# Two waits of a fused attention and feed-forward kernel made finer: the value product by channel block, the bias by head group

## The reference

```python
x = x + tanh(g_xattn) * attention(layernorm(x), ctx)     # 16 heads of 32 channels, ALiBi bias, exp / (1 + sum)
# feed-forward of the RWKV kind, on h = layernorm(x)
xr = mu_r * h + (1 - mu_r) * h_prev ; xk = mu_k * h + (1 - mu_k) * h_prev
r = sigmoid(xr @ W_r.T) ; k_act = square(relu(xk @ W_k.T))
x = x + tanh(g_ffn) * r * (k_act @ W_v.T)
```

## Time and profile before

| | us |
|---|---|
| median of 3 runs | 1499.18 |
| lowest and highest | 1497.6, 1499.49 |
| the profiled execution | 1499.1 |
| its span, first to last instruction | 1497.3 |
| outside the span | 1.8 |

### The profile page before, as it was taken

One profiled execution on the slowest core, in us unless ns is written; L12 is line 12 of the kernel. 1 busy time (PEld: TensorE's weight loads), 2 busy tenths in 40 slices (PEclk: granted clock), 3 DMA queues, 4 the chain that ended last, 5 costly groups with the idle time before them and its releaser, 6 DMA issues.

```text
span 1497.3 us, 32734 instructions
## 1 busy us (share of the span) xinstructions
PE 1358.7 (91%) x10864; PEld 1122.8 (75%) x10864; DVE 1161.3 (78%) x2889; ACT 878.0 (59%) x2928; POOL 722.2 (48%) x766
## 2 busy tenths in 40 slices
PE   7988899899989999999998989998898999889898
PEld 6877778677777877778786777777686777768677
DVE  4447868787887878798786879878687987868785
ACT  5247474655747475574747566473756657375662
POOL 0003465545545554545555465555556454555542
PEclk9999999999999999999999999999999999999999
DMA  8721001020101102010010202011020101011000
GB/s 271 213 75 46 12 29 51 0 77 0 57 21 28 49 0 77 0 57 21 28 49 9 68 0 57 21 37 40 14 63 0 57 21 57 21 28 50 1 30 28
DMA packets 53009, 65.95 MB, mean 44 GB/s; under 512 B 23024, under 2 KB 29168, under 8 KB 52976
## 3 DMA queue, kind: packets, MB, share of 16 engines
q1 hardware_dynamic: 52976, 65.52, 14.9%
HBM read 40.87 MB, written 24.64 MB: 44 GB/s over the span
## 4 chain that ended last, share of the span: by engine, by line
DVE 37%; PE 22%; issue 21%; POOL 9%; ACT 6%; DMA 4%; DVEq 1%; SPq 1%; POOLq 0%; ACTq 0%
PE rotating L402 16%; DVE probs L1043 7%; DVE diff L1105 4%; POOL square L1362 4%; DVE mix_k L1100 4%; PE score_bank L402 3%; DMA xs<-in_x_dram 3%; DVE square L1100 2%; DVE relu L1105 2%; DVE xs L1069 2%; DVE mask_in L1142 2%; DVE stats L1013 2%; POOL probs L1325 2%; ACT probs L778 2%; DVE norm L1022 2%
## 5 line engine op out<-in xcount | busy, mean ns | idle before, releaser
L778 ACT ACTIVATE probs<-probs,neg_max 128x120 f32<-128x120 f32 x1024 | 391.7, 387 | 32.9 <-DVE neg_max L1047 32.9
L1325 POOL TENSOR_TENSOR probs<-probs,recip 128x960 f32<-128x960 f32 x128 | 229.8, 1795 | 216.2 <-DVE recip L1058 216.2
L402 PE MATMUL rotating<-mixed_key,w_key 128*128 128x512 f32 x720 | 202.6, 431 | 43.2 <-ACT gated L830 43.2
L402 PE MATMUL rotating<-w_proj,attn_t 128*128 128x512 f32 x768 | 199.7, 406 | 20.7 <-ACT gated L830 18.7
L1043 DVE SCALAR_TENSOR_TENSOR probs<-mask_in,score_bank 128x120 f32<-128x120 f32 x1024 | 213.5, 270 | 0.0
L402 PE MATMUL rotating<-w_value,xnt_or_act 128*128 128x512 f32 x720 | 187.8, 403 | 18.2 <-DVE xs L1069 13.1
L402 PEld LDWEIGHTS rotating<-mixed_key,w_key 128*128 128x128 f32 x720 | 140.9, 204 | 82.7 <-ACT gated L830 49.6
L402 PE MATMUL rotating<-xnt_or_act,w_query 128*128 128x256 f32 x1536 | 198.7, 286 | 0.5 <-DVE xnt_or_act L1028 0.5
L778 ACT ACTIVATION_READ_ACCUMULATOR probs<-probs,neg_max 128x1 f32 x1024 | 195.6, 191 | 0.0
L402 PE MATMUL rotating<-w_gate,mixed_gate 128*128 128x512 f32 x768 | 189.8, 399 | 0.0
L402 PEld LDWEIGHTS rotating<-xnt_or_act,w_query 128*128 128x128 f32 x1536 | 187.7, 191 | 1.9 <-DVE xnt_or_act L1028 0.8
(11 more groups left out here) (129 smaller groups left out, 2334.1 us busy)
## 6 DMA issues: line engine op xcount, KB each, us to landing
xs<-in_x_dram SPq DMA_DIRECT2D x64, 256.0 KB, 2.9
out_dram<-gated SPq DMA_DIRECT2D x64, 256.0 KB, 3.0
value_scratch<-gated SPq DMA_DIRECT2D x16, 240.0 KB, 2.6
mask_in<-in_mask_dram SPq DMA_DIRECT2D x16, 240.0 KB, 2.6
keys_t<-key_scratch SPq DMA_DIRECT2D x16, 240.0 KB, 3.5
values<-value_scratch SPq DMA_DIRECT2D x16, 240.0 KB, 3.8
probs<-in_ctx_t_dram SPq DMA_DIRECT2D x6, 480.0 KB, 6.6
key_scratch<-query_t SPq DMA_DIRECT2D x12, 240.0 KB, 4.5
```

Of the source, the lines that this page charges most:

```text
L402: mm = pe.matmul(bank, stationary(a, c), moving(b, c), start=(i == 0), stop=(i == MATMULS - 1))
L778: e = act.activation(probs[:, t % 2, head, :], probs[:, t % 2, head, :], ACT.Exp, bias=neg_max[:, t % 2, head:head + 1], accum_out=sums[:, ...
L1325: pool.tensor_tensor(part, part, recip[:, t % 2, heads].unsqueeze(2).to_broadcast((P, H // 2, NK)), ALU.mult)\
```

## The change

`value` now issues its matmuls one at a time and, for tile 0, waits at the first pass of each channel block c until that block's low part is there: four waits, for one block, two, three and four, in place of one for four. `bias` drops the wait on exp_done; the wait on probs_turned is now made for every head group g, for the turning of group g of tile t - 2 alone. All else, the order on every engine too, stays.

```diff
             def value(b, t, steps, banks=bank_of):
-                if t == 0 and steps[0] == 0:
-                    pe.wait_ge(act_low, (b + 1) * CT)
-                return product(banks["value", t][:], lambda s, c: xnt_or_act[:, s, c, t * P:(t + 1) * P],
-                               lambda s, c: w_value[:, s, c, :], steps)
+                for step in steps:
+                    c, first = divmod(step, len(SPLIT_PASSES))
+                    if t == 0 and first == 0:
+                        pe.wait_ge(act_low, b * CT + c + 1)
+                    mm = product(banks["value", t][:], lambda s, c: xnt_or_act[:, s, c, t * P:(t + 1) * P],
+                                 lambda s, c: w_value[:, s, c, :], [step])
+                return mm
...
                     dve.wait_ge(scores_done, b * QT + t + 1)
                     if t == 0:
                         dve.wait_ge(dist_ready, b + 1)
-                    if earlier(b, t, 2):
-
-                        dve.wait_ge(probs_turned, (b * QT + t - 1) * G)
-                        dve.wait_ge(exp_done, (b * QT + t - 1) * G)
+                if earlier(b, t, 2):
+
+                    dve.wait_ge(probs_turned, (b * QT + t - 2) * G + g + 1)
                 for j in range(J):
```

## The result

| | median, us | runs from, to | ratio to before, 95% interval |
|---|---|---|---|
| before | 1498.39 | 1496.71, 1499.49 | |
| after | 1508.78 | 1507.96, 1509.41 | 1.007 [1.0053, 1.0087] |

The change makes the kernel 10.4 us slower. The forecast was 1495.5 us, 3.6 us faster, and the range ended at 1499.6. A case that ended slower was among the rivals, but the profile shows that it is not the mechanism that it named.

The account below looks back on a forecast made before the run. PE's savings were taken to count only where they reach DVE: 0.27 us gained less 0.03 for the bias is 0.24 in each of 15 rounds, 3.6 us off 1499.1, giving 1495.5 us; range 1493.7 to 1499.6.

Parts of the forecast that it names:

- What bounds the kernel: Whole round: PE's saved time counts only where it reaches DVE; 0.52 us on PE become 0.27 on DVE.
- The value product: PE, tile 0: the stall on POOL's low part goes whole; PE gains about 0.52 us a round.
- POOL as what is late next: Third turning of tile 1: POOL's second half holds it, so it moves by only 0.36 us.
- the 0.13 us of the earlier trace: A PE turning that waits for POOL starts 0.13 us after POOL's end.
- three waits that cost nothing that shows: PE's added waits in the value product: taken as 0, upper end 0.24 us a round.
- the middle, 0.27: DVE's reciprocals of tile 2: gain a round, taken between 0.23 and 0.31 us.
- The bias, price of the waits: DVE: changed waits of the bias cost 0.03 us a round, with no gain from finer waiting.
- The pairs of 0.57 us: DVE behind a maximum: next start 0.57 us later with or without a wait, so a met wait is free.
- that of 0.12: DVE bias without a wait, 0.12 us behind a reciprocal; expected to grow to at most 0.20.
- the pair of 0.20: DVE bias with three waits starts 0.20 us behind a reciprocal, so three waits cost 0.08 us.
- the bounds of -0.05 and 0.16: Bias on DVE: limits in us a round around the forecast cost of 0.03.
- Rival (b): DVE, groups 1 to 3 of tiles 2, 3 and 0: nine new waits cost 0.08 us each; 1505.9 us, chance 0.08.

Follow-up runs that it names:

- the value edit alone: Kernel before with only the finer waits of `value`, `bias` unchanged: 1494.14 us, ratio 0.9969.
- both edits and 31 ahead: Kernel after with 31 one-column writes to an unused tile at the start of DVE's list, before the loop: 1495.05 us.
- 48 ahead: Kernel after with 48 one-column writes to an unused tile at the start of DVE's list, before the loop: 1495.79 us.

## Why the prediction was wrong, step by step

- **What bounds the kernel** was right: PE gained 0.51 us in the round shown and DVE 0.31 of it, and the mean round of the value edit alone is 0.30 us shorter.
- **The value product** was right in each step: 0.52 forecast and 0.51 measured on PE, POOL as what is late next with the 0.13 us of the earlier trace rows, three waits that cost nothing that shows (the product lasts 2.91 us with them, 2.99 without). Of 0.23 to 0.31 a round the middle, 0.27, had been taken; the mean round says 0.30, the whole time of the value edit alone, 4.1 us, says 0.27.
- **The bias, price of the waits**, was right in that it is next to nothing. The pairs of 0.57 us are unchanged, and so is that of 0.12 for which 0.04 had been taken; the pair of 0.20 fell to 0.17 (timeline of after above). The mean round is 0.02 us longer with both edits and 31 ahead than with the value edit alone, and 0.10 longer with 48 ahead: within the bounds of -0.05 and 0.16. As the waits are the same in both, the 0.08 between the two is not their price, and no run says what it is.
- **The step that failed** is the last sentence of that part: "The registers in which the loop works out the thresholds are more by a few on both engines; the instructions in front are long enough to hide them, and without that cover they are inside the bounds." I costed these instructions by the time in which they are issued, and did not count them by the room that they take. The bias edit adds five to the DVE loop, and the loop had room for two. That term of the sum, taken as 0, is +14.7 us of idle time. (PE's loop gained none, so "on both engines" was wrong as well.)
- **Rival (b)** named the right sign and the right edit, with 6.8 us, and the wrong mechanism: nine places of 0.08 us. The rows show one place of 1.13. That its time, 1505.9, is near the measured one is chance.
- **The sum with the missing term**: 1495.5 + 14.7 = 1510.2, measured 1508.78. In a round it closes: 86.47 - 0.30 + 1.13 of stall + 0.08, by which DVE's instructions otherwise overlap at that place too, = 87.38, as measured. The 13 rounds are 13 x 0.91 = 11.8 us longer, the profiled spans only 1506.2 - 1497.3 = 8.9: the start is 0.9 us shorter in after and the end 2.0, of which the gains of the last two rounds are 0.6. The rest is what starts and ends differ by in the other runs too (first bias of batch 1 at 180.0 to 182.6 us).

The Trainium skill has a rule that bears on this, which I had not weighed. Runtime: NRT & Kernel Launch, section Instruction fetch mechanics, says that a taken branch whose target is not in the window that is loaded forces a fetch of it before execution goes on. The trace agrees: 2.8 us from the branch to the loop's first instruction, and 14.7 / 13 = 1.13 us of idle time ahead of the first bias of a round. The same section gives blocks of 16 KiB, 256 instructions, and two of them in an engine. On DVE the packets here are of 8.2 KB and come 128 instructions apart, and the measurement decides; the times alone would not have told the two sizes apart.

The signs that could have been read beforehand: in the page of before, q14 has 14 packets in the whole span, so that the loop over the batches stays loaded, and nothing said how near to the edge it was. A change that adds register thresholds inside such a loop puts this at risk, and the right forecast would have been two cases with a real chance for each: 1495.5, and a slower one whose price no row of before could give.

## What to carry to other kernels

Count instructions as room, not only as time: where an engine runs a long loop, compare its length in the compiled program before and after an edit, and look at the instruction queues in the DMA part of the page; packets that grow with the number of rounds mean that the loop is fetched anew. A loop's place matters as much as its length: five instructions ahead of it cost 16 us here, and 31 ahead of the changed one gave 14 us back. Such a gain hangs on the exact count of instructions, so that the next edit ahead of the loop or in it can take it away. A finer wait is worth its instruction only where the coarse one is late: here one was (4.1 us), and the other was met before by the order of the engine's own list, so there was nothing for it to gain.

## What the runs showed of the hardware

- DVE's instructions come in packets of 8.2 KB on q14, one for every 128 instructions (in a round of after the last three start when 31, 152 and 281 of its 287 instructions have; shifts of 24 and 31 instructions give 1538.5 and 1495.05 us).
- In all runs here, a loop of DVE that touches three blocks is not fetched again (14 or 15 packets in the span), and one that touches four is fetched whole in each round, five packets with the block behind it. From the branch to the loop's first instruction it is then 2.8 us where it is 0.3 otherwise, and DVE is idle for 1.13 us of it in the mean. In the one run in which the first block has only four instructions of the loop left, there is a second stop of 1.77 us in the mean.
- The fetch hardly shows in the busy shares or in the times of DMA work (q14 has 0.1% of the engines' time): it shows as idle time with the releaser "issue", and in the count of packets.
- A met wait on DVE costs nothing behind a maximum of 0.65 us (0.57 us from start to start, with it and without); behind a reciprocal of 0.20 us, in the lines shown, one wait costs nothing (0.12 both ways), two cost 0.05 and three 0.08.
